# A segment sum over sorted edges with a two-layer network: one loop over all laps, GpSimd's x sums ahead of its powers, longer runs in the edge loads from earlier steps on

## The reference, cut to what matters

```python
col = edge_index[1]                                    # = dst, sorted ascending
agg = segment_sum(edge_attr, col, num_segments=6250)   # 200000 x 128 f32 -> 6250 x 128
h = concatenate([x, agg, u[batch]], axis=1)            # batch is all zeros: one row of u
h = relu(h @ W1 + b1)
out = layernorm(x + (h @ W2 + b2))                     # over the 128 features, eps 1e-5
```

## Time and profile before

| | |
|---|---|
| time, median of 3 runs | 275.75 us (275.32 to 275.93) |
| profiled execution | 276.12 us, span 274.4 us |
| bytes moved by DMA | 110.06 MB, mean 401 GB/s |
| PE busy | 213.2 us (78%), mean granted clock 0.938 |
| VectorE (DVE) busy | 177.2 us (65%) |
| ScalarE (ACT) busy | 50.8 us (19%) |
| GpSimd (POOL) busy | 41.5 us (15%) |

### The profile page before, as it was taken

One profiled execution on the slowest core, in us unless ns is written; L12 is line 12 of the kernel. 1 busy time (PEld: TensorE's weight loads), 2 busy tenths in 40 slices (PEclk: granted clock), 3 DMA queues, 4 the chain that ended last, 5 costly groups with the idle time before them and its releaser, 6 DMA issues.

```text
span 274.4 us, 15313 instructions
## 1 busy us (share of the span) xinstructions
PE 213.2 (78%) x6767; PEld 168.7 (61%) x6767; DVE 177.2 (65%) x435; ACT 50.8 (19%) x100; POOL 41.5 (15%) x49
## 2 busy tenths in 40 slices
PE   0874899987886449999884789895898897867872
PEld 0763687855655347877653658674766676655751
DVE  7842285793674997596874436959928769465542
ACT  0410122311211201122210211322022212121210
POOL 6400020030210012040300200300303003030020
PEclk9998699999999859999999599999599999999997
DMA  7999999999999999999999999999999999999994
GB/s 252 391 396 401 400 401 404 402 401 405 402 406 402 401 402 402 404 401 415 416 418 409 416 412 414 421 415 416 418 426 428 422 425 432 418 430 422 429 393 174
DMA packets 28863, 110.06 MB, mean 401 GB/s; under 512 B 2008, under 2 KB 3374, under 8 KB 26926
## 3 DMA queue, kind: packets, MB, share of 16 engines
q1 hardware_dynamic: 25588, 105.83, 95.9%
q10 hardware_dynamic: 3258, 4.00, 4.0%
HBM read 106.63 MB, written 3.20 MB: 400 GB/s over the span
## 4 chain that ended last, share of the span: by engine, by line
PE 58%; issue 13%; DVE 12%; DMA 12%; POOL 1%; ACT 1%; DVEq 1%; POOLq 0%; ACTq 0%
PE rows_ps L860 31%; PE cols_ps L872 14%; DMA slots<-in_edge_attr 12%; PE hid_ps L904 4%; PE hid_ps L886 3%; DVE tall_ids L687 3%; PE hid_ps L895 3%; PE hid_ps L880 2%; ACT rows L444 1%; DVE hot L615 1%; DVE z L678 1%; DVE first_of_pair L570 1%; POOL rstd L408 1%; DVE dst_local L583 1%; DVE high L696 1%
## 5 line engine op out<-in xcount | busy, mean ns | idle before, releaser
L860 PE MATMUL rows_ps<-slots,hot 64*32 64x128 f32 x6240 | 113.4, 285 | 35.7 <-issue 23.4
L860 PEld LDWEIGHTS rows_ps<-slots,hot 64*32 64x32 f32 x6240 | 93.6, 110 | 53.5 <-issue 50.7
L641 DVE TENSOR_TENSOR agg_t<-agg_t,cols_ps 128x128 f32 (+1 forms) x65 | 21.5, 331 | 84.1 <-PE cols_ps L872 83.8
L872 PE MATMUL cols_ps<-row_hot,rows 128*128 128x128 f32 (+1 forms) x260 | 56.3, 341 | 11.4 <-ACT rows L444 6.3
L615 DVE TENSOR_TENSOR hot<-edge_node,iota 128x768 f32<-128x768 f32 x65 | 61.8, 952 | 2.5 <-issue 1.6
L444 ACT ACTIVATE rows<-rows_ps 128x256 f32<-128x256 f32 x65 | 25.0, 384 | 177.3 <-PE rows_ps L860 170.1
L872 PEld LDWEIGHTS cols_ps<-row_hot,rows 128*128 128x128 f32 x260 | 40.8, 198 | 25.3 <-ACT rows L444 13.1
L408 POOL TENSOR_TENSOR rstd<-var_eps,minus_half 128x4 f32<-128x4 f32 (+1 forms) x13 | 16.6, 1275 | 196.7 <-DVE var_eps L672 196.7
L631 DVE TENSOR_TENSOR row_hot<-row_node,iota 128x256 f32<-128x256 f32 (+1 forms) x65 | 38.4, 591 | 0.0
L399 POOL TENSOR_TENSOR z<-x_rows,b_all 128x512 f32<-128x512 f32 (+1 forms) x13 | 17.2, 1323 | 29.8 <-PE hid_ps L880 29.8
L678 DVE TENSOR_SCALAR z<-z,moments,rstd (+1 forms) x49 | 17.2, 410 | 1.1 <-POOL rstd L408 1.0
(11 more groups left out here) (119 smaller groups left out, 70.3 us busy)
## 6 DMA issues: line engine op xcount, KB each, us to landing
slots<-in_edge_attr SPq DMA_DIRECT2D x65, 1536.0 KB, 14.9
x_rows<-in_x ACTq DMA_DIRECT2D x11, 256.0 KB
out<-z SPq DMA_DIRECT2D x11, 256.0 KB
dst_int<-in_dst SPq DMA_DIRECT2D x1, 384.0 KB, 3.9
dst_int<-in_dst ACTq DMA_DIRECT2D x1, 384.0 KB, 4.6
x_rows<-in_x ACTq DMA_DIRECT2D x1, 192.0 KB
out<-z SPq DMA_DIRECT2D x1, 192.0 KB
rest_slot<-in_edge_attr ACTq DMA_DIRECT2D x1, 128.0 KB, 8.5
```

Source lines behind the costliest of these rows:

```text
L641: V.tensor_tensor(cols, cols, cols_ps[:, 0:n], ALU.add).then_inc(added, 1)
L860: done = T.matmul(rows_ps[i][c * SPAN:(c + 1) * SPAN, h, 0:feats], hot[j][part, c * RUN + r, :], slots[part, j, c, r * feats:(r + 1) * fea ...
L872: done = T.matmul(cols_ps[:, 0:n], rows[i][:, h, :], row_hot[j][:, h, 0:n], start=(h == 0), stop=(h == HALVES - 1))
```

## The change

- `DENSE` goes from step 30 to step 25 and `TALL` from step 50 to step 48: five steps get runs of 6144 instead of 3072 bytes, two steps 12288 instead of 6144.
- PE and VectorE get one loop for all laps. Each step has 224 columns in `level2`, `row_hot` and `add`; only the very last step has 128 in `level2` and `add`. PE runs `level1(t)`, then `level2(t-1)`, except at the fifth step of a lap (j = 4), where `level2(t-1)` comes before `level1(t)`, because steps 3 and 4 of a lap now share one buffer (`SETS` = 0, 1, 0, 1, 1).
- There are two `rows_ps` sets instead of three. The PSUM space goes to banks of their own for turned x (`turn_bank`) and y (`y_bank`), so `turn_x` no longer waits for `z_made`. `turn_x` moves to the second step of a lap (j = 1) and `product1_x` to the third (j = 2). The filler matmul of the last lap is gone.
- POOL runs bias_add(0), bias_add(1), and then each power before the bias_add two blocks on. It also clears `x_rows` once at the start, and the first `load_x` waits for that.
- ScalarE copies rows of step t at its own place in every lap, runs `relu` and `copy_x` at j = 1 and `load_x` at j = 3.
- The blocks are shifted by 128 nodes: the block in pieces is now the first (block 0), and block 11 is a plain block.
- `judge`'s count is read out by VectorE into `bad_total` at lap 9; PE no longer waits for `plan_made`.

```diff
-SETS = (0, 1, 0, 1, 2)
-DENSE_LAP = 6
-DENSE = DENSE_LAP * LAP
-TALL = 10 * LAP
+SETS = (0, 1, 0, 1, 1)
+DENSE = 5 * LAP
+TALL = 48
...
+        top_rows = ROWS - 1
+        top_parts = nodes - FIRST - (blocks - 1) * BLOCK - top_rows * P
+        top_even = top_parts // 16 * 16
...
+    def start_of(i):
+        return 0 if isinstance(i, int) and i == final else FIRST + (blocks - 1) * BLOCK - i * BLOCK
...
-        rows_ps = [pb(f"rows_ps{i}", [P, HALVES, 512]) for i in range(3)]
+        rows_ps = [pb(f"rows_ps{i}", [P, HALVES, 512]) for i in range(2)]
         cols_ps = pb("cols_ps", [P, 512])
-
+        turn_bank = pb("turn_bank", [P, BLOCK])
         hid_ps = pb("hid_ps", [P, BLOCK])
-        y_ps = hid_ps[:, :].rearrange("p (r f) -> p r f", r=ROWS)
-        turn_ps = y_ps
+        y_bank = pb("y_bank", [P, BLOCK])
...
+            G.memset(x_rows[:, :, :], 0.0).then_inc(x_zero, 1)
...
             bias_add(0, 0)
+            bias_add(1, 1)
             for i in range(places):
                 reciprocal_deviation(i, i)
-                if i + 1 < places:
-                    bias_add(i + 1, i + 1)
+                if i + 2 < places:
+                    bias_add(i + 2, i + 2)
...
             for lap in range(laps):
-                dense_lap = lap >= DENSE_LAP
                 for j in range(LAP):
                     t = lap * LAP + j
-
-                    if dense_lap:
+                    if t:
                         copy_rows(t)
-                    elif t + 1 < DENSE:
-                        copy_rows(t + 1)
-                    if j == 0 and lap:
-                        relu(lap - 1)
-                    elif j == 3:
+                    if j == 1:
+                        if lap:
+                            relu(lap - 1)
                         copy_x(lap)
-                    elif j == 4 and lap < final:
+                    elif j == 3 and lap < final:
                         load_x(lap + 1)
...
+            def one_lap(lap):
+
                 at = counts(lap)
-                for j in range(LAP):
+                for j in range(-1, LAP - 1):
                     t = lap * LAP + j
+                    if j == 0:
+                        with dve.If(lap == JUDGE + 1):
+
+                            dve.wait_ge(bad_summed, 1)
+                            dve.wait_ge(level2_done, t + 1)
+                            V.tensor_copy(bad_total[:, :], bad_ps).then_inc(bad_read, 1)
+                            dve.wait_ge(bad_read, 1)
+                    add(t, at[j + 1], COLS)
                     if j == 1:
                         residual(lap - 1, lap - 1)
+                        with dve.If(lap == TURN):
+                            turn_tall_ids()
                         with dve.If(lap == JUDGE):
                             judge()
...
-            def dense_lap(lap):
+            def one_lap(lap):
                 counts(lap)
                 for j in range(LAP):
                     t = lap * LAP + j
                     if j == 4:
-                        with pe.If(lap == JUDGE + 1):
-
-                            pe.wait_ge(plan_made, 1)
-                        with pe.If(lap > final - 1):
-                            product1_x(final, final)
-
-                            pe.wait_ge(rows_copied, laps * LAP)
-                            T.matmul(rows_ps[SETS[j]][:, 0, feats:512], ident[:, :], iota[:, feats:512], start=True, stop=True)
+
+                        level2(t - 1, j - 1, COLS)
                     level1(t, lap, j)
+
                     if j == 0:
...
+                    elif j == 1:
+                        with pe.If(lap > 0):
+                            pe.wait_ge(added, lap * LAP + 1)
+                            product1_agg(lap - 1, start_of(lap - 1))
...
+                        level2(t - 1, j - 1, COLS)
+                        turn_x(lap, lap * 16 + x_landed(0, 0))
+                    elif j == 2:
+                        with pe.If(lap > 0):
+                            product2(lap - 1, lap - 1)
+                        level2(t - 1, j - 1, COLS)
+                        product1_x(lap, BLOCK)
                     elif j == 3:
...
+                        level2(t - 1, j - 1, COLS)
...
-            with pe.Fori(0, DENSE_LAP) as lap:
-                sparse_lap(lap)
-            level2(DENSE - 1, LAP - 1, False)
-            with pe.Fori(DENSE_LAP, laps) as lap:
-                dense_lap(lap)
+            with pe.Fori(0, laps) as lap:
+                one_lap(lap)
+            level2(held, LAP - 1, DENSE_COLS)
```

More of the change, by code:

```diff
@@ L173, in residual_gnn_layer @@
         row_hot = [sb(f"row_hot{i}", [P, HALVES, COLS]) for i in range(HOTS)]
[L174 removed]
+        rows = [sb(f"rows{i}", [P, HALVES, feats]) for i in range(2)]
         agg_t = sb("agg_t", [P, width])
@@ L782, in _ @@
             V.tensor_tensor(agg_t[:, 0:SPAN], agg_t[:, 0:SPAN], hid_ps[:, 0:SPAN], ALU.add).then_inc(added, 1)
-            sparse_lap(0)
-            with dve.Fori(1, DENSE_LAP) as lap:
-                sparse_lap(lap)
+            first_at = step_bases(0, LAP - 1)
+            for t in range(LAP - 1):
+                add(t, first_at[t], COLS)
+                make_hot(t + AHEAD, t + AHEAD)
+            dve.wait_ge(wide_ids_copied, SHARE)
             dve.wait_ge(first_in, 16)
             V.tensor_copy(edge_node[:, held, :, :].rearrange("p c r -> p (c r)"), first_int[:, :])
-            with dve.Fori(DENSE_LAP, laps) as lap:
-                dense_lap(lap)
+            with dve.Fori(1, laps) as lap:
+                one_lap(lap)
+            add(held, 0, DENSE_COLS)
             residual(final, final)
```

219 lines of the change are left out of this document (69 added, 150 removed).

## The result

| | before | after |
|---|---|---|
| time, median | 275.36 us (6 runs) | 277.43 us (6 runs, 277.0 to 278.39) |
| profiled execution | 276.12 us, span 274.4 us | 277.31 us, span 275.6 us |
| PE busy, clock | 213.2 us, 0.938 | 219.0 us, 0.95 |
| VectorE busy | 177.2 us | 191.6 us |

The ratio is 1.0066 with a 95% interval of 1.0047 to 1.0085. The forecast was faster, 274.4 us. Every ratio here is formed from the executions within 1.5% of their kernel's fastest, and not from the two medians, so it can differ a little from their quotient (here 1.0075).

A forecast was written before the change was run, and what follows sets the result against it. The prediction took gapless loads plus a fixed 9.0 us tail to bound the kernel. Its terms -0.79, -1.1 and +0.5 summed to -1.4 us, giving 274.4 us by the median, with an 8 in 10 range of 273.5 to 276.5.

The forecast's parts named there:

- What bounds the kernel: Whole kernel: loads run without a gap and a fixed tail follows; time is the last landing plus 9.0 us.
- Term 1: Loads of steps 25 to 29 and 48, 49: longer runs raise the DMA rate, -0.79 us.
- rival 3: Loads: run length does not set the rate, stages differ by when they run; 275.15 us, chance 0.07.
- Term 2: Landings 19 to 54: code packets at PE's second loop entry cause a slip; one loop removes it, -1.1 us.
- Rival 1: Landings 19 to 54: the 1.1 us slip stays, caused by a remaining packet; 275.5 us, chance 0.17.
- The turn of the tall indices: Lap 3, VectorE: PE some 3 us later, but loads issued five steps ahead keep the queue full; no cost.
- Term 3: PE's steady laps: wider columns and a serial place, 16.6 us a lap against 19.1 of loads; hidden, nothing.
- Term 4: Last lap: the serial place makes level1(64) start 0.5 us late, unhidden; bounds 0 and 1.2.
- rival 2: After judge: PE late at the end, deciding from 18.1 us a lap; 277.2 us at 3.70 a step, chance 0.16.
- The end, at nothing: Last store: stores stay behind all loads on SP's queue and the last waits for VectorE; no change.
- At nothing, the rest: Remaining edits, such as POOL's bias_add order (its products due a lap later) and judge's count readout; no cost.
- Rival 4: PE's loop: a lap's code outgrows the store and each lap stops; 295 us or more, chance 0.02.

The follow-up runs named there:

- a_best2: a_delay with product1_x of the last block moved behind the loop; 276.06 us against 276.07 for the kernel before, ratio 0.9996.
- a_late: a_nofallall with VectorE waiting at its very end until all stores have landed; 277.5 us, ratio 1.0053.
- a_delay: a_nofallall with two small multiplications on VectorE between its last normalise and its reading of the plan; 276.84 us, ratio 1.0021.
- a_again: The changed kernel unchanged, run again for reference and a second profile; 277.51 us, ratio 1.0067.
- a_px: The changed kernel with product1_x of the last block taken behind the loop, 128 columns wide; 277.06 us, ratio 1.0042.
- a_nofall: The changed kernel with the never-entered fallback path left out on VectorE only; 277.28 us, ratio 1.005.
- a_nofallall: The changed kernel with the never-entered fallback path left out on all five engines; 277.59 us, ratio 1.0067.
- a_best: a_late with product1_x of the last block moved behind the loop; 276.59 us, ratio 1.0025.
- b_early: The kernel before, with VectorE reading the plan before the last block's residual instead of behind its normalise; 276.58 us against 275.79, ratio 1.0026.
- a_split: The changed kernel with PE's one loop written twice, laps 0 to 5 and 6 to 12; 284.4 us, ratio 1.0307.
- a_poolold: The changed kernel with GpSimd's order of before (bias_add of the next block after each power); 294.04 us, ratio 1.0554.

## Why the prediction was wrong, point by point

**What bounds the kernel**: half right. The last landing and the tail behind it make the time, but the tail is not fixed: the prediction had 9.0 us from the last landing to the end, and it was 9.1 before and 11.4 after.

**Term 1**, -0.79: right as far as it can be told. The runs alone gave -0.7, with an interval that just touches none. Steps of 3072 byte runs land 3.91 us apart, of 6144 3.77 and of 12288 3.69, where no x is between, and five and two such steps make 0.9. This speaks against rival 3.

**Term 2**, -1.1: right in the slip and in that it goes with the second loop, wrong in which packets cause it. The slip can be found. In the kernel before the load of step 41 was issued at 166.30 and that of step 42 at 169.36; the DMA view for the two issues gives (last number: us to landing)

```profile
slots<-in_edge_attr SPq DMA_DIRECT2D x1, 1536.0 KB, 9.5
...
slots<-in_edge_attr SPq DMA_DIRECT2D x1, 1536.0 KB, 11.9
```

so 5.5 us lie between their landings, where 3.77 and one block of x (0.63) make 4.4. The 1.1 us over are as long as the packet of 16 KB of instructions at 177.5 us took, 1.11. In the changed kernel, where that packet is missing, the two landings are 3.77 apart (issued at 158.67 and 162.55):

```profile
slots<-in_edge_attr SPq DMA_DIRECT2D x1, 1536.0 KB, 17.8
...
slots<-in_edge_attr SPq DMA_DIRECT2D x1, 1536.0 KB, 17.7
```

The four packets of PE's second loop, which I blamed, lie between 137 and 157 us, and the eleven steps from 29 to 40 took 42.6 us with two blocks of x in them, which is 11 x 3.77 and 2 x 0.63 to 0.1 us: they cost nothing. The fifth is there in every kernel with a second loop of PE and in none with one loop. That it makes the slip is read from a coincidence in all four profiles with PE's order of before, not shown by taking it away alone: the step in which it ends takes 5.5, 5.6, 5.0 and 5.3 us from the landing before (in the last, the kernel with the runs alone, this is step 43, in the others 42), 0.6 to 1.2 over 4.4. What the gain is worth can be read from landing 28 to landing 64: 140.1 us with the runs alone, 138.6 to 139.2 in the nine profiles of the changed kernel and of its variants that leave PE's loop and GpSimd's order as they are. Rival 1, that the slip stays, is out. Against the runs alone only 0.1 us of earlier last landing remains all the same (264.17 against 264.31). From landing 29 to 45 the changed kernel is 0.8 faster, but step 0 lands 0.3 later on average (9.8 to 10.1 us in the twelve kernels with the change, 9.5 to 9.8 in the four without), and 0.2 is lost after step 54. The cleared x_rows and the two further pieces of block 0, which I put at nothing, are the likely cause of the late start; no run takes one of them away.

**The turn of the tall indices, at nothing**: this step failed too, and none of the experiments was made for it. I gave PE 3 us of lateness and said that loads issued five steps ahead would cover it. But level1 of step 19 stands behind level2(18) at the serial place, and that waits for an add behind the turn:

```profile
98.25 1.83 PE L859 MATMUL cols_ps<-row_hot,rows 128*128 128x224 f32 x4 [9.73 <-DVE agg_t L633]
```

Level1 of step 19 began at 100.01, 10.5 us behind its landing and 10.9 later than before. The load of step 24 waits for it and was issued 3.6 us before step 23 landed, where it had been 13.9. The DMA view for 100 to 110 us, in slices of 0.25 us: before, after, and a_best2.

```profile
GB/s 393 418 406 406 406 406 418 418 393 393 406 406 393 406 381 418 406 393 393 393 406 393 393 406 406 393 406 418 406 430 406 393 406 385 377 418 377 438 406 446
```

```profile
GB/s 406 393 393 393 418 418 393 406 393 406 393 393 356 344 295 221 160 184 258 295 381 406 393 393 393 430 418 455 406 406 406 406 418 479 455 418 430 442 393 442
```

```profile
GB/s 393 418 393 393 406 393 406 393 406 406 406 393 393 393 221 172 147 221 197 147 197 283 344 369 418 430 319 270 356 393 406 406 430 442 418 406 406 467 442 516
```

In the changed kernel's first profile, in a_late and in a_delay the load (issued 3.6, 2.9 and 3.4 us ahead) came just in time, step 24 landed 3.9 us after step 23, and the last landing is at 264.2. In the six other profiles with this order of the loads (a_again, a_px, a_nofall, a_nofallall, a_best, a_best2) the load came 2.3 to 2.9 us ahead, step 24 landed 0.3 to 1.4 us late, and the last landing is at 264.8 to 265.6, in part for other reasons. Over the nine profiles the lateness of step 24 is 0.45 us on average, a cost that none of the experiments takes away.

**Term 3**, PE's steady work at nothing: right in the result outside lap 3, for the wrong size. Five steps of lap 9 and 10 with no load awaited take 221.12 - 203.64:

```profile
203.64 1.59 PE L847 MATMUL rows_ps<-slots,hot 64*32 64x128 f32 x96
...
211.09 0.99 PE L859 MATMUL cols_ps<-row_hot,rows 128*128 128x224 f32 x4 [0.68 <-DVE agg_t L633]
...
214.53 1.58 PE L847 MATMUL rows_ps<-slots,hot 64*32 64x128 f32 x96 [0.92 <-DVE hot L619]
...
221.12 1.59 PE L847 MATMUL rows_ps<-slots,hot 64*32 64x128 f32 x96
```

17.5 us, where I took 16.6: VectorE's one-hot tiles are late by 0.9 once and by 0.2 once, and the wait at the serial place is 0.68. PE is back on the landings at step 56, as in the kernel before at step 54. The rival's point, 18.1 us a lap, was not reached by the changed kernel, but the serial place moved by one step reaches it.

**Term 4**, the tail at +0.5: this is the step that failed. The serial place is priced rightly, 4.15 us from level1 of 63 to that of 64 in both. But I let it start at the landing of step 63, and it starts 0.79 us behind it, since the step before holds level1, product2, a level2 of 224 columns and a product1_x of 512 columns for a block that has 128: 261.21 - 256.98 = 4.23 us against landings 3.69 apart. I had checked a lap's sum against 19.1 us of loads and never the single steps of the last lap. +1.1 in place of +0.5. This is rival 2's end without its cause: PE was late at step 64 by its last lap, not by judge.

**The end, at nothing**: the second step that failed, and the larger one. "The last store waits for VectorE" is true and the store's issue was on time, 272.13. Its landing was not, 1.0 us late, with a fetch of instructions beside it that no row of a duration shows. The sum took it as given that the time from the store's issue to its landing stays. b_early makes it in the kernel before, +0.8, and a_delay takes it away in the changed kernel, -0.75 (spans +0.75 and -1.1). What the trace does not say is which of the 16 engines a packet is on; that both are on the same one is inferred from the store's last 8 packets of 128, which in all eleven profiles with a late store start within 0.02 us of the end of the instruction packet. That the packet is VectorE's is inferred too, from the two experiments that move it. Open is what decides the order of the two. By the record the packet starts 1.03 to 1.16 us behind the store's issue in the kernels with a late store and 1.47 in those without, but with the fallback left out on VectorE alone it starts at 1.46 and the store is late all the same. VectorE's own late end adds up to 0.3 us to the span, which left out alone gave nothing measurable.

**At nothing, the rest.** Whether GpSimd's order is worth nothing as a gain no run shows, but "due a lap later" was wrong: it carries the moved turn_x. The copy of judge's count left no cost that the rows show. Rival 4, code that does not stay, is out: five packets on q8 for thirteen laps.

In sum, with sizes from the experiments and profiles: runs -0.7, one slip of 1.1 less, late start and last steps +0.5, step 24 +0.45 on average, tail +1.1, last store +0.7 to +1.0, VectorE's end up to +0.3. That is +1.0 to +1.6, of the 1.65 to 2.1 measured; the rest is not assigned. My forecast had the gains nearly right, and of the costs only 0.5 of some 3 us.

## What to carry to other kernels

A lap's sum shows whether an engine keeps up; whether a change shows at the end is decided by the single steps of the last lap, so lay them out one by one against the landings, with everything that the loop still issues there for a block that no longer needs it. The same goes for a lap with extra work in it: ask how long before the landing ahead of it the next load is issued, and not only how many loads are queued. A change in the order of one engine's instructions shifts when its code is fetched, and at the very end of this kernel, where a small store is all that is awaited, one 8 KB fetch was worth some 0.75 us, so compare the gap from the last store's issue to its landing before believing a result below 0.5%. And when a consumer is moved to an earlier step, follow every producer's queue back: GpSimd's order looked free, and the moved turn_x could not do without it: 16.5 us by the medians.

## What the runs showed of the hardware that I had not expected

- A packet of 8 KB of instructions (0.3 to 0.7 us) at about the time of a 64 KB store of 512 byte rows goes with one sixteenth of that store coming 0.3 to 0.6 us late, and its landing from 1.5 to 1.8 us after the issue to 2.4 to 2.8. The late part was there in 11 profiles, in 10 of them with the packet 1.03 to 1.16 us behind the store's issue and in one with 1.46; it was absent in the three with 1.47, where the store's data had gone through, and in the two in which the packet had come 0.6 and 0.8 us ahead of the issue (a_best2, a_delay).
- Waiting on a semaphore seems not to keep an engine from fetching what follows: with VectorE at a wait for the last store from 272.91 on, the packet still came at 273.33, 1.09 us after the store's issue (a_late). That it is VectorE's is inferred.
- Of five 16 KB packets between 137 and 179 us, each some 1.1 us long, four left the landings where they were, and the step in which the fifth ends landed 0.6 to 1.2 us late, in all four profiles with PE's order of before.
- The 1.5 MB load of step 24 landed on time when it was issued 3.4 us or more before the landing ahead of it; issued 2.3 to 2.9 us ahead it was on time once and 0.3 to 1.4 us late eight times, a_split and a_poolold among them. The rate fell to under 200 GB/s for 0.5 us in the changed kernel's profile and for 1.25 us in that of a_best2.
